# A grouped-query attention step: transposed scores issued ahead of the plain scores in every round

## The reference

```python
def xattn(q, k, v, Wq, Wk, Wv, Wfc, bfc):       # 32 heads of 16, 8 key/value groups
    qh = (q @ Wq.T) -> (8, 32, 256, 16); kh, vh = (k @ Wk.T), (v @ Wv.T) -> (8, 8, 256, 16), each for 4 heads
    score = einsum('bhqd,bhkd->bhqk', qh, kh) / sqrt(16)
    out = einsum('bhqk,bhkd->bhqd', softmax(score), vh)
    return out.reshape(8, 256, 512) @ Wfc.T + bfc
def ffn(x):
    comb_w = sum of the softmax of the top 2 of x @ router.T      # 8 experts
    return mlp(x, shared 2048) + mlp(x, routed 256) * comb_w      # mlp: silu(x@g.T) * (x@u.T) @ d.T
x = x + tanh(g_xattn) * xattn(layernorm(x), ctx, ctx, ...)
x = x + tanh(g_ffn) * ffn(layernorm(x))
```

## Time and profile before

| | us |
|---|---|
| median of 3 runs | 889.69 (889.41 to 889.77) |
| profiled execution, its own time | 890.05 |
| its span, from the first to the last instruction | 887.7 |
| PE busy | 860.1 |
| DVE busy | 635.8 |
| ACT busy | 337.2 |
| POOL busy | 477.8 |

### The profile page before, as it was taken

One profiled execution on the slowest core, in us unless ns is written; L12 is line 12 of the kernel. 1 busy time (PEld: TensorE's weight loads), 2 busy tenths in 40 slices (PEclk: granted clock), 3 DMA queues, 4 the chain that ended last, 5 costly groups with the idle time before them and its releaser, 6 DMA issues.

```text
span 887.7 us, 14887 instructions
## 1 busy us (share of the span) xinstructions
PE 860.1 (97%) x4923; PEld 642.5 (72%) x4923; DVE 635.8 (72%) x1085; ACT 337.2 (38%) x636; POOL 477.8 (54%) x485
## 2 busy tenths in 40 slices
PE   8689999999999889999999999999999999999998
PEld 6445665665565447888888888888788888888886
DVE  7789899889889966666556655679665566656565
ACT  4186576667657852122112211344211121112111
POOL 2313004001203999787668666954966696678640
PEclk9889999999999999999999999999999999999999
DMA  7763342432432113121112111211311112111102
GB/s 274 232 175 105 127 121 61 149 116 78 131 107 74 38 28 93 48 72 47 47 47 71 47 47 47 72 47 65 115 59 48 47 52 66 47 47 47 47 1 95
DMA packets 43609, 71.88 MB, mean 81 GB/s; under 512 B 6064, under 2 KB 21936, under 8 KB 43312
## 3 DMA queue, kind: packets, MB, share of 16 engines
q1 hardware_dynamic: 43568, 71.34, 25.5%
HBM read 55.33 MB, written 15.73 MB: 80 GB/s over the span
## 4 chain that ended last, share of the span: by engine, by line
PE 84%; DVE 11%; issue 2%; ACT 1%; DMA 1%; SPq 0%; DVEq 0%; ACTq 0%
PE bank L1293 24%; PE bank L1295 23%; PE bank L1294 23%; DVE mcol L906 5%; PE bank L1353 4%; PE bank L1378 4%; PE bank L1368 3%; PE bank L1298 2%; PE bank L1399 1%; DVE oN L1038 1%; ACT probs L761 1%; DVE oB L1028 1%; DVE x_l L1256 1%; DVE aT_l L881 0%; DMA q_scr<-qx_l 0%
## 5 line engine op out<-in xcount | busy, mean ns | idle before, releaser
L1293 PE MATMUL bank<-x_l,w_h 128*128 128x512 f32 x504 | 197.3, 391 | 0.3 <-DVE c L1116 0.3
L1294 PE MATMUL bank<-x_h,w_l 128*128 128x512 f32 x504 | 196.2, 389 | 0.0
L1295 PE MATMUL bank<-x_h,w_h 128*128 128x512 f32 x504 | 196.2, 389 | 0.0
L906 DVE TENSOR_REDUCE mcol<-bank 128x2 f32<-128x512 f32 x256 | 164.7, 671 | 24.8 <-PE bank L1353 24.3
L620 ACT ACTIVATE hT_h<-bank 128x512 fp32r<-128x512 f32 x72 | 43.1, 599 | 355.9 <-DVE bank L1231 347.2
L761 ACT ACTIVATE probs<-bank 128x512 f32<-128x512 f32 x256 | 138.9, 596 | 73.3 <-PE bank L1368 71.7
L572 POOL TENSOR_TENSOR w_l<-raw,w_h 128x512 fp32r<-128x512 f32 (+1 forms) x144 | 161.9, 1157 | 2.9
L1128 DVE SCALAR_TENSOR_TENSOR xa<-bank,tgf,xa 128x512 f32<-128x512 f32 x128 | 96.2, 751 | 77.7 <-PE bank L1295 77.5
L1293 PE MATMUL bank<-dn_l,hT_h 128*128 128x512 f32 x288 | 112.0, 389 | 0.0
L1294 PE MATMUL bank<-dn_h,hT_l 128*128 128x512 f32 x288 | 112.0, 389 | 0.0
L1295 PE MATMUL bank<-dn_h,hT_h 128*128 128x512 f32 x288 | 112.0, 389 | 0.0
(11 more groups left out here) (149 smaller groups left out, 1340.6 us busy)
## 6 DMA issues: line engine op xcount, KB each, us to landing
raw<-w_gu SPq DMA_DIRECT2D x36, 512.0 KB, 3.3
dnraw<-w_dn SPq DMA_DIRECT2D x36, 256.0 KB, 2.6
q_st<-q_scr SPq DMA_DIRECT2D x64, 128.0 KB, 2.7
q_scr<-qx_h SPq DMA_DIRECT2D x16, 256.0 KB, 2.2
q_scr<-qx_l SPq DMA_DIRECT2D x16, 256.0 KB, 2.2
q_st<-q_scr SPq DMA_DIRECT2D x64, 64.0 KB, 2.7
out<-xa SPq DMA_DIRECT2D x16, 256.0 KB, 2.0
cx_raw<-ctxT SPq DMA_DIRECT2D x14, 256.0 KB, 3.0
```

The source lines that it names most:

```text
L906: v.tensor_reduce(at[:, :, qt], sm_bank(n, s, u)[:, :].rearrange("p (r k) -> p r k", r=2), AX.X, ALU.max).then_inc(max_ok, 1)
L1293: mm(out, a_h, b_l, start=start, stop=False, skip_group_check=onto)
L1294: mm(out, a_l, b_h, start=False, stop=False, skip_group_check=onto)
L1295: return mm(out, a_h, b_h, start=False, stop=stop, skip_group_check=onto)
```

## The change

Within a round, `st_pair` of step n goes ahead of `sm_pair` of step n + 2, with its own wait for `m_rd` in round 0. The waits for `q_rd` and `k_rd` stay with the plain scores, now behind. Nothing else is changed.

```diff
                     look = not last or e < STEPS
                     for v in range(UNITS // 2):
+                        if v == 0:
+                            pe.wait_ge(m_rd, 32 * (n + 1))
+                        st_pair(n, v, bb, c)
                         if look:
                             if v == 0:
                                 pe.wait_ge(q_rd[ce], 64 * (2 * te + be + 1))
                                 pe.wait_ge(k_rd[be], 64 * (te + 1))
                             sm_pair(n + 2, e % STEPS, v, be, ce)
-                        if v == 0:
-                            pe.wait_ge(m_rd, 32 * (n + 1))
-                        st_pair(n, v, bb, c)
                         if v == 0 and not (first and s == 0):
                             for p in (2, 3):
                                 pv_unit(n - 1, p, (s - 1) % STEPS // CHUNKS, (s - 1) % CHUNKS)
```

## The result

The changed kernel takes 890.75 us (median of 20 runs, 890.13 to 891.90), the kernel before 889.38 in the same session (20 runs, 887.47 to 890.31). The ratio is 1.0019, 95% interval 1.0012 to 1.0025: slower by 1.1 to 2.2 us. Predicted were +1.1 us and 890.8.

The account below looks back on a forecast made before the run. PE was taken as the bound, busy 97% of the span, with DVE-full stretches in the attention steps. Terms 0.3 + 1.24 - 0.2 - 0.23 = +1.1 us on 889.69 gave 890.8; eight times in ten 888.2 to 893.0.

Parts of the forecast that it names:

- (a): Undisturbed rounds: ACT's loop 1.67 us against PE's 1.66 to 1.68, so nothing or 0.01 in some 30 rounds, +0.3.
- (b): Rounds where ACT is late: plain scores now stand behind the wait instead of in its shade, +0.23 us.
- (c): Step 3 of pairs 1 and 2 and the release in step 4: earlier POOL adds shorten DVE's divide, -0.24 us together.
- Step 1: Pairs 1 and 2: filler later behind the release at 203.21, +0.22 us, and behind the one of 207.54, +0.20.
- Step 2: Pairs 1 and 2: ACT's excess no longer covered by plain scores, +0.20 us, and +0.08 in its second half: +0.28.
- Step 3: Pairs 1 and 2: divide ends 0.24 us earlier and PE's filler starts a further 0.23 earlier, -0.47.
- Step 4: Pairs 1 and 2: release of 230.39 loses 0.23 us by (b); second half, behind the query copy, +0.16.
- (d): Pair 0: most of DVE's loss of up to 0.97 us falls into a later stall; -0.2, bounds -0.6 and +1.0.
- slower rival: DVE starved as plain scores stand behind the wait for an exponential, mainly step 1 of pair 0: +3.0 us, 892.7; chance 0.32.
- (e): Pair 3: transposed scores go into PE's 1.09 us idle time at step 5's end, -0.23; earlier DVE waits cancel.
- The wait for m_rd: Wait for the maxima's copy, moved ahead of plain scores: costs nothing; uncovered, up to 0.34 us in each of 32 steps.
- faster rival: Transposed scores no longer stand behind a maximum, each of 12 DVE waits saves 0.23 us: -2.0, 887.7; chance 0.17.

Follow-up runs that it names:

- e10: New order with DVE's transpose (L1028) moved ahead of the second maximum of its step: rounds 1 to 2 of step 2 take 2.58 us instead of 2.81.
- e0: The kernel before, unchanged, profiled and timed again: ratio as expected (1.000 within 0.001), span 886.9 us.
- e2: Kernel before with the new order in pair 0 alone: pair 0 takes 79.46 us against 78.95.
- e3: Kernel before with the new order in pair 3 alone: 0.62 us gained before its last transposed scores, in whole about -0.2.
- e1: Kernel before with the new order in pairs 1 and 2 alone: middle pairs 74.27 and 74.26 us against 73.58.
- e5: New order, with POOL's bias adds in pairs 1 and 2 delayed until step 4's exponentials are done: middle pair 74.00 us.
- e9: Kernel before with the new order in pairs 0 and 3, and POOL's bias adds delayed as in e4: middle pairs 72.91 and 72.94 us.
- e6: Kernel before with the new order in rounds 1 and 3 alone: +3.1 us per pair, +0.9% in all.
- e7: Kernel before with the new order in rounds 0 and 2 alone: middle pairs 74.03 and 74.31 us.
- e4: Kernel before, old order, with POOL's bias adds in pairs 1 and 2 delayed until step 4's exponentials are done: middle pair 72.92 us.

## Why the prediction was right

**The pair of groups** is 0.66 where 0.67 was taken. (It changes places 120 times, not 124: the last eight rounds have no plain scores. The sum doesn't use the number.) **(a)** gave what was said: three undisturbed steps (5 to 7) of pair 2 grow by 0.09.

**(b) and (c), steps of pair 2.** Step 1, the rows after of both releases, the exponentials between, and the filler's weight load, beside the earlier trace rows:

```profile
203.30 0.50 PE L1368 MATMUL bank<-q_st,k_st 49*128 49x512 f32 x2 [0.69 <-ACT probs L761]
...
206.65 1.07 ACT L761 ACTIVATE probs<-bank 128x512 f32<-128x512 f32 x2
...
207.78 0.50 PE L1368 MATMUL bank<-q_st,k_st 49*128 49x512 f32 x2 [0.64 <-ACT probs L761]
...
208.44 0.19 PEld L1293 LDWEIGHTS bank<-wfc_l,aT_h 128*128 128x128 f32 x1
```

Related to the pair's opening the first release stays (+0.02), and the filler follows after 0.66 where it was 0.44; the exponentials of 206.34 are at 206.65, 0.24 later on the same scale (0.15 said). Step 1: +0.45 (0.42 predicted).

Step 2 has the right sum for a partly wrong reason. Rows: transposed scores of round 1, DVE's transpose, the filler's last matmul, the turn of the maxima.

```profile
212.20 0.50 PE L1368 MATMUL bank<-q_st,k_st 49*128 49x512 f32 x2
...
213.04 0.71 DVE L1028 STREAM_TRANSPOSE oB<-bank 128x512 f32<-128x512 f32 x1
...
213.43 0.39 PE L1295 MATMUL bank<-wfc_h,aT_h 128*128 128x512 f32 x1
...
213.89 0.27 PE L1298 MATMUL bank<-ident,mcol 128*16 128x128 f32 x1
```

Here round 1 comes 212.20 - 210.46 = 1.74 after round 0, where PE would be free at 1.66, so ACT's excess is 0.07 and not the 0.20 of the prediction. The other 0.17 is the turn of the maxima, 0.46 behind the filler, because DVE's transpose ends about then (e10). Step 2: +0.24 (0.28 predicted).

Step 3 and the release in step 4, beside the earlier trace rows: DVE's first maxima, POOL's adds, the divide, the last plain scores, the release.

```profile
221.10 1.29 DVE L906 TENSOR_REDUCE mcol<-bank 128x2 f32<-128x512 f32 x2 [1.24 <-PE bank L1353]
...
223.78 5.20 POOL L480 TENSOR_TENSOR xa<-xa,tbias 128x512 f32 x4
...
224.21 1.14 DVE L1038 TENSOR_TENSOR oN<-oB,rden 128x256 f32<-128x256 f32 x1
...
226.46 0.50 PE L1353 MATMUL bank<-k_st,q_st 48*128 48x256 f32 x4
...
230.71 0.49 PE L1368 MATMUL bank<-q_st,k_st 49*128 49x512 f32 x2 [0.48 <-ACT probs L761]
```

The adds start 0.25 earlier against the step's opening, the divide takes 1.14 (1.1 said), and PE's filler starts 226.46 + 0.44 = 226.90, which is 0.46 earlier against the step's opening (0.47 said). Step 3: -0.47. The release of 230.71 has its plain scores behind it: +0.24, with 0.06 for the second half of the step, where I had 0.16. Step 4: +0.30.

Over the eight middle pairs of before, e0, e2 and e3 and the four of after and e1, the means of steps 0 to 4, and of 5 to 7 together, differ by +0.03 + 0.47 + 0.25 - 0.48 + 0.31 + 0.08 = 0.66; predicted were 0.62 and the pair's share of (a).

**(d) pair 0** is the term that was off, small as it is: +0.2 to +0.5 for -0.2. That the round opens 0.60 us later (the first transposed scores wait for all 16 maxima of two steps, `max_ok`, 2 * UNITS, the plain scores only for 15) costs nothing by itself, since the transposed scores start where they did. But their plain scores now come behind them, and DVE gets them later. From half a microsecond into the run of eight to the end of the DVE-full stretch, DVE's waits for plain scores are, before and after:

```profile
DVE mcol L906 <- PE bank L1353: 4.5, 5, 1.6
...
DVE mcol L906 <- PE bank L1353: 5.5, 7, 1.3
```

So DVE was starved, as the slower rival had it and as the prediction's own sign asked ("new idle time in pair 0 before L906"), and from step 0 on. It was 1.04 us late at the low part of the attention output, against the loss of up to 0.97 said, and this stall took most of it, as (d) had said: it takes 0.42 for the 1.47 of the earlier trace rows. After the next such stall 0.05 was left, up to the end of the stretch. The rows: the filler at that end before; then the low part, and plain scores and filler at that end, after.

```profile
83.48 0.50 PE L1293 MATMUL bank<-xnT_l,wq_h 128*128 128x512 f32 x1
```

```profile
62.21 0.42 DVE L881 TENSOR_TENSOR aT_l<-aT,aT_h 128x256 fp32r<-128x256 f32 x1
...
82.12 0.50 PE L1353 MATMUL bank<-k_st,q_st 48*128 48x256 f32 x4
...
82.55 0.50 PE L1293 MATMUL bank<-xnT_l,wq_h 128*128 128x512 f32 x1
```

From the run's start the plain scores are at 42.97 for 42.92, and the filler at 43.40 for 43.58: -0.18. The 0.23 came; the 0.14 "from earlier copies" did not, and is what (d) had mis-sized most. The second half of step 4 gives +0.24 (0.16 said), and from there to the end of the pair it is another 0.10, of the kind of (a). In all +0.16.

In e2, e5 and e9 DVE is 0.27 to 0.37 us late at the end of the stretch instead of 0.05, and all behind it is alike. There PE's granted clock fell to its lower level (0.50, that is 1.2 GHz) in step 1, where it stayed at the upper one (1.00, 2.4 GHz) in the profile after. The same 3 us, counted from the run, in e2 and after (the third number from the right is the granted clock):

```profile
57.70:60.70 3.00, 3.00 (x26) 1.40 (x24) 2.29 (x5) 2.50 (x7) 0.45 (x1) 0.50 0.39 105
```

```profile
58.18:61.18 3.00, 2.51 (x30) 1.48 (x31) 2.82 (x6) 3.00 (x7) 0.24 (x2) 1.00 0.41 98
```

DVE then idles 1.08 us for plain scores in e2, and 0.15 after. So the fall goes with the spread of pair 0 from +0.2 to +0.5. In steps 1 and 2 of pair 0 it is in five of the eight profiles that have the new order in some rounds there (e2, e5, e6, e9, e10) and in none of the six others. PE had been busy 4.32 of the 6.0 us before it in e2, and 4.33 in the same stretch after, where it didn't fall; what brings it is open.

**(e) pair 3**: -0.2 predicted; -0.6 up to the last transposed scores, and 0.3 to 0.5 of it lost behind them. Step 5 gives -0.24, the 0.23 said. Steps 1 and 2 gain 0.2 each as well, where the prediction let the earlier waits for DVE cancel: in step 1, too, the transposed scores now go into a wait for a maximum (0.46 us before). So (d) came out 0.4 higher and (e), with the rest, 0.2 lower; that the sum, 1.1, meets the +1.05 of the profiles so closely is partly luck, while the middle pairs, most of the sum, are right by their mechanism.

**The wait for m_rd** shows in one place after, as 0.4 us of weight-load idle time that the matmuls before it cover; it was nearer than I thought (e7). The slower rival had the right engine but not the price: in the middle pairs late maxima cost through DVE's transpose in step 2, and in pair 0 the later stall takes them up. The faster rival is refuted by the sum of PE's waits: those for maxima went down by 5.3 us, those for ACT and for DVE's transpose up by 4.8 and 1.4. Its mechanism is what pair 3 shows.

## What to carry to other kernels

When two groups that wait for different engines change places, give each engine's loop its time from the opening of the round to the next release: here 1.67 against 1.66 us decided that nothing was lost in most rounds. Then look only at rounds where one of the two is late: what stands ahead of a wait is covered by it, what stands behind is added. Look also at what else waits for the result that now comes later, in every step and not only where DVE is full. A round that opens later costs nothing if the group that the next engine waits for starts where it did. For effects near a microsecond, compare a repeating period in the profiles and not the span, and look at the granted clock before two profiles are compared.

## What was not expected of the hardware

The start of the kernel, up to the same run of maxima, differs by 1.75 us between 14 profiles (38.67 to 40.42), while a middle pair of one order repeats within 0.06; that can be a good part of the spread of the times (887.5 to 890.3 for one kernel), which was not traced. A divide takes 0.41 us alone, and 1.14 or 1.54 when it is issued beside POOL's adds, by where in the first add that is. PE's granted clock fell to 0.50 for about 3 us in pair 0 in five of 14 profiles; three of them can be compared with profiles of the same order without it, and are 0.2 to 0.3 us longer in that pair. The Trainium skill (SBUF — State Buffer, "SBUF: two separate sides") has the port as held for a whole instruction; e4 and e5 agree, with 0.66 and 0.42 us per pair.
